# Placing the values of a second attention: by token and 25 small DMAs, or by a block-diagonal copy, transposes and small copies

## What is computed

```python
x = x + tanh(g_xattn[0]) * L0_xattn(layernorm(x), ctx, ctx, mask)     # 16 heads of 64
x = x + tanh(g_ffn[0])   * L0_ffn(layernorm(x))                       # 3 cycles of a coupling net
x = x + tanh(g_xattn[1]) * L1_xattn(ctx, layernorm(x), mask)          # 16 heads of 16
x = x + tanh(g_ffn[1])   * L1_ffn(layernorm(x))                       # shared expert + top 2 of 8 experts

def L1_xattn(src, tgt, attention_mask, Wq, Wk, Wv, Wo):
    q = heads(tgt @ Wq.T); k = heads(src @ Wk.T); v = heads(src @ Wv.T)
    scores = where(attention_mask, q @ k.T / sqrt(16), -inf)
    return merge(softmax(scores) @ v) @ Wo.T
```

## Time and profile before

| | us |
|---|---|
| median of 3 runs | 793.06 (792.92 to 800.51) |
| the profiled execution | 793.08, of which the span of its instructions is 791.3 |
| busy in the span: PE | 750.0 |
| PEld | 507.1 |
| DVE | 413.3 |
| ACT | 253.2 |
| POOL | 120.4 |

### The profile page before, as it was taken

The page is one execution under the profiler, slowest core; times in us unless marked ns, Lnnn a source line. Parts: engine busy times, 40 slices in busy tenths (PEclk is TensorE's granted clock), DMA queues, the critical chain, the costliest instruction groups (busy, mean ns, idle before and its releaser), DMA issues. The chain is left out here.

```text
span 791.3 us, 11353 instructions
## 1 busy us (share of the span) xinstructions
PE 750.0 (95%) x3378; PEld 507.1 (64%) x3379; DVE 413.3 (52%) x987; ACT 253.2 (32%) x542; POOL 120.4 (15%) x129
## 2 busy tenths in 40 slices
PE   7989999999899998799999999999999999999992
PEld 6856677667654444578888856556566566566661
DVE  5868766677723667976766635122333333333340
ACT  1532222222344444456566522111112122121220
POOL 4100000000000000000000103660132232322322
PEclk9999999999999999999999999999999999999996
DMA  9444000000032000047000201222223223232221
GB/s 304 132 135 136 0 0 1 0 0 0 1 119 94 0 1 0 1 167 260 0 0 1 81 1 69 101 100 74 42 40 48 46 43 50 40 47 47 41 39 20
DMA packets 38720, 45.09 MB, mean 57 GB/s; under 512 B 4212, under 2 KB 32454, under 8 KB 38692
## 3 DMA queue, kind: packets, MB, share of 16 engines
q1 hardware_dynamic: 31348, 34.99, 14.0%
q0 software_dynamic: 7344, 9.75, 7.5%
HBM read 27.91 MB, written 16.79 MB: 56 GB/s over the span
## 5 line engine op out<-in xcount | busy, mean ns | idle before, releaser
L399 PE MATMUL ps<-middle,work 128*128 128x256 f32 (+3 forms) x824 | 217.7, 410 | 2.2 <-ACT work L956 1.5
L956 ACT ACTIVATE work<-ps 128x256 f32<-128x256 f32 (+5 forms) x276 | 99.1, 412 | 364.9 <-PE ps L402 344.6
L399 PEld LDWEIGHTS ps<-middle,work 128*128 128x128 f32 x824 | 152.1, 190 | 42.5 <-issue 23.6
L399 PE MATMUL ps<-early,work 128*128 x312 | 141.1, 595 | 0.8 <-ACT work L956 0.8
L402 PEld LDWEIGHTS ps<-consts_sb,work 128*128 128x128 f32 (+1 forms) x672 | 76.7, 140 | 47.8 <-issue 26.4
L399 PE MATMUL ps<-late,work 128*128 128x34 f32 (+5 forms) x576 | 102.8, 331 | 3.6 <-ACT work L956 3.6
L402 PE MATMUL ps<-consts_sb,work 128*128 128x128 f32 (+1 forms) x672 | 93.8, 276 | 11.9 <-ACT work L956 4.7
L399 PEld LDWEIGHTS ps<-early,work 128*128 128x128 f32 x312 | 57.8, 190 | 61.7 <-issue 60.5
L399 PEld LDWEIGHTS ps<-late,work 128*128 128x128 f32 x576 | 81.2, 191 | 18.0 <-issue 8.9
L363 POOL TENSOR_TENSOR rstd<-var_eps,minus_half 128x8 f32<-128x8 f32 (+2 forms) x8 | 13.4, 1671 | 433.0 <-DVE var_eps L1266 433.0
L399 PE MATMUL ps<-early,late 128*128 128x512 f32 (+2 forms) x192 | 78.9, 615 | 0.0
(11 more groups left out here) (158 smaller groups left out, 607.1 us busy)
## 6 DMA issues: line engine op xcount, KB each, us to landing
early<-in_w SPq DMA_DIRECT2D x16, 512.0 KB, 10.1
expert_rows<-work SPq DMA_DIRECT2D x39, 130.0 KB, 2.7
work<-expert_rows SPq DMA_DIRECT2D x39, 130.0 KB, 2.1
middle<-in_w SPq DMA_DIRECT2D x8, 512.0 KB, 8.3
x_rows<-in_x SPq DMA_DIRECT2D x4, 512.0 KB, 9.6
out_rows<-x_rows SPq DMA_DIRECT2D x4, 512.0 KB, 3.4
late<-in_ws SPq DMA_DIRECT2D x3, 512.0 KB, 4.5
early<-in_wv SPq DMA_DIRECT2D x1, 1024.0 KB, 9.1
```

The lines of the kernel that those rows point to most:

```text
L399: return nc.tensor.matmul(o, l, r, start=start, stop=stop, **kw)
L956: return nc.scalar.activation(o, i, ACT.Copy)
```

## The change

The value projection is computed with tokens on the partitions (77 rows, 2 x 256 columns, bank 7), DVE copies it in one instruction to `vtok` (region `work`, 77 rows), and SP moves the rows of each head to their place in `va` by 25 DMAs (one for each head, and one more wherever a head crosses a chunk's end), both batches in one. POOL zeroes `va` in setup, and DVE waits for that before it writes the ones. PE's wait on `su1_t` becomes waits on `ones_done` and on all 25 DMAs. The block-diagonal copy, its memsets, the transposes and ACT's copies are gone. The 25 DMAs stand on SP behind the loads of `w2s` and ahead of those of `w13`.

```diff
@@ block.sync, after the loads of w2s
+            sp.wait_ge(q["su1_dve"], 2)
+            for h in range(H):
+                for c in range(NK * h // P, (NK * h + NK - 1) // P + 1):
+                    a, z = max(NK * h, P * c), min(NK * h + NK, P * c + P)
+                    sp.dma_start(va[a - P * c:z - P * c, :, c, h - heads_of(c)[0], 0:HD],
+                                 vtok[a - NK * h:z - NK * h, :, HD * h:HD * h + HD]).then_inc(q["ld_va"], 16)
@@ block.gpsimd, after the memset of mlhs
+            nc.gpsimd.memset(va.rearrange("p b c h e -> p (b c h e)"), 0.0).then_inc(q["va_fill"], 1)
@@ block.tensor, su1(w)
-                for m in range(2):
-                    for k in range(KD):
-                        last = mm(ps[:, 7, PW * m:PW * m + PW], (wk1s, wv1s)[w][:, k, P * m:P * m + P], ctx[:, k, :],
-                                  k == 0, k == KD - 1)
+                if w == 0:
...
+                else:
+                    for b in range(B):
+                        for k in range(KD):
+                            last = mm(ps[0:NK, 7, D * b:D * b + D], ctx[:, k, NK * b:NK * b + NK], wv1s[:, k, :],
+                                      k == 0, k == KD - 1)
@@ block.tensor, behind the net
             net3(5)
-            pe.wait_ge(q["su1_dve"], 2)
-            su1_turn(0)
             to_rows(1, 0, 4)
             to_rows(1, 1, 5)
             net4(5)
-            su1_turn(1)
...
-            pe.wait_ge(q["su1_t"], B * KC)
+            pe.wait_ge(q["ones_done"], B)
+            pe.wait_ge(q["ld_va"], 16 * (H + KC - 1))
@@ block.scalar
             act3(5)
-            act.wait_ge(q["ones_done"], B)
-            su1_turned(0)
             act4(10)
-            su1_turned(1)
             act4(11)
@@ block.vector
+            dve.wait_ge(q["va_fill"], 1)
             for b in range(B):
                 v.tensor_copy(va[:, b, :, :, HD], ...
@@ block.vector, su1_build(w)
+                else:
+                    last = v.tensor_copy(vtok.rearrange("p b d -> p (b d)"), ps[0:NK, 7, :])
@@ block.vector, in the loop of updates
                 if n == 3:
                     su1_build(0)
-                    for a, z in ((0, ZL), (ZL + HALF, Z1)):
-                        seq.mark(v.memset(z1[:, :, :, a:z], 0.0))
                 if n == 5:
-                    seq.sync()
                     su1_build(1)
```

More of the change, by code:

```diff
@@ L25 @@
 ZN = PAIRS * ZS + P
-ZL = 104
-Z1 = ZL + HALF + 48
 G4 = 512
@@ L105, in after @@
         eng.wait_ge(sem, value)
-def halves_of(c):
-    h0, n = heads_of(c)
-    return sorted({h0 // 8, (h0 + n - 1) // 8})
 def quarters(ap):
@@ L172, in build @@
         zv = cut(early, 8192 + B * PAIRS * PW, [B, ZN])
-        z1 = cut(work, 1536, [B, 2, Z1])
+        vtok = cut(work, 1536, [B, D])[0:NK]
         w13 = cut(early, 0, [NE, 2, KD, F])
@@ L248, in build @@
         dve_seq act_seq pool_seq var_done rstd_done memset_done gate_done
-        su_mm su_kv su_crow su_crow_bf su_g_mm su_g su_v_mm su_v bo_done ones_done su1_mm su1_dve su1_tm su1_t mask_done mrow_done
+        su_mm su_kv su_crow su_crow_bf su_g_mm su_g su_v_mm su_v bo_done ones_done su1_mm su1_dve va_fill ld_va mask_done mrow_done
         seed_mm seed_row n_xn n_tx n_xt n_sc n_sub n_exp n_p n_tp n_pt n_pv n_res
@@ L460, in su1 @@
                 pe.wait_ge(q["f_a4"], 2 * w + 3)
-                for m in range(2):
-                    for k in range(KD):
-                        last = mm(ps[:, 7, PW * m:PW * m + PW], (wk1s, wv1s)[w][:, k, P * m:P * m + P], ctx[:, k, :],
-                                  k == 0, k == KD - 1)
-                last.then_inc(q["su1_mm"], 1)
[L467 to L475, removed]
+                if w == 0:
+                    for m in range(2):
+                        for k in range(KD):
+                            last = mm(ps[:, 7, PW * m:PW * m + PW], wk1s[:, k, P * m:P * m + P], ctx[:, k, :],
+                                      k == 0, k == KD - 1)
+                else:
+                    for b in range(B):
+                        for k in range(KD):
+                            last = mm(ps[0:NK, 7, D * b:D * b + D], ctx[:, k, NK * b:NK * b + NK], wv1s[:, k, :],
+                                      k == 0, k == KD - 1)
+                last.then_inc(q["su1_mm"], 1)
             def xt(i, k, pre):
@@ L980, in _ @@
                                      ACT.Copy, scale=gate[:, 0:1]).then_inc(q["su_v"], 1)
[L982 to L992, removed]
             def ev_xt(i, k, pre, used):
@@ L1336, in su1_build @@
                 dve.wait_ge(q["su1_mm"], w + 1)
[L1337 to L1342, removed]
+                if w == 0:
+                    src = ps[:, 7, 0:2 * PW].rearrange("p (m b t) -> p m b t", m=2, b=B)
+                    for b in range(B):
+                        for m in range(2):
+                            last = v.tensor_tensor(kb1[:, b, m, :].rearrange("p (h t) -> p h t", h=8),
+                                                   spread(src[:, m, b, :], 1, [P, 8, NK]),
+                                                   spread(con[:, C_BD:C_BD + 8], 2, [P, 8, NK]), ALU.mult)
+                else:
+                    last = v.tensor_copy(vtok.rearrange("p b d -> p (b d)"), ps[0:NK, 7, :])
                 last.then_inc(q["su1_dve"], 1)
```

## The result

| | before | after |
|---|---|---|
| median, us | 793.08 (790.77 to 801.01, 20 runs) | 800.9 (795.04 to 805.34, 20 runs) |
| profiled execution, us (span) | 793.08 (791.3) | 801.58 (799.6) |
| granted TensorE clock over the span, its share of full speed | 0.990 | 0.973 |

The ratio is 1.0063, 95% interval 1.0039 to 1.0088: slower, by less than 1%. The medians differ by 7.8 us and the means by 5.6, since each kernel's runs fall into groups with different clocks. The forecast was 791.15 in a range of 788.5 to 794.2.

A forecast was written before the change was run, and what follows sets the result against it. PE was taken as the bound, busy 95% of the span, but in the seam PE's late `to_rows(1, 0)`, then DVE. Terms -2.23 - 0.40 + 0.70 = -1.93 took 793.08 to 791.15 us, range 788.5 to 794.2.

The forecast's parts named there:

- DVE's gap, -2.23: Seam, 304 to 317: DVE's idle time before `ffn_out(1, 0)` goes, since PE does `to_rows(1, 0)` earlier; -2.23 us.
- The second gap, -0.40: Before 323.74: DVE's idle time waiting for `to_rows(2, 0)` on PE closes; -0.40 us.
- `su1(1)`, +0.70: Value projection in the net: eight records of 256 instead of 154 columns, where PE has no slack; +0.70 us.
- DVE's copy at 0.75 us: Net: DVE's one 77x512 copy takes 0.75 us, all covered by PE, so it costs 0.
- The memset at 0.9 us: Setup: POOL zeroes `va` in 0.9 us, ending at 10.4; DVE comes at 19.57, so it costs 0.
- The 25 DMAs: On idle SP: 0.49 us per issue, last down at 295.5, PE needs them at 314.0; cost 0.
- The rival of late rows: Seam: uneven spread over engines makes PE wait for the DMAs at 314.0; decides from 64 ns per packet; chance 0.06.
- the cover of 1.6 us: Seam: PE's first scores are ready 1.6 us before DVE's softmax asks; without it the gain shrinks one for one.
- the price taken: DMAs landing late in the seam at 93 ns per packet, half way between 57 and 129: 14.2 us late, 803.8 us.
- The whole passage: Rival, seam: both turns leave PE, 3.16 us each, and all of it is gained: 787.5 us; chance 0.07.
- the swallowed gain: Rival, first tiles: PE's waits for ACT grow by what is gained, leaving 793.8 us; sign: longer waits; chance 0.13.
- The forecast's own range: Range of the main forecast, 789.8 to 793.0, said to come from the value projection's bounds and 1.6 us cover; chance 0.74.

The follow-up runs named there:

- e2_fill_two: Changed kernel plus 22 useless TensorE transposes behind `net4(5)` and 14 more behind `to_rows(2, 1)`, in the next hole: 797.8 us, ratio to before 1.0036.
- e1_fill: Changed kernel plus 22 useless TensorE transposes of the identity matrix behind `net4(5)`, in the 3.32 us hole: 795.4 us, ratio to before 1.0005.
- e6: Kernel before plus two useless matmuls of 208 columns (0.7 us) behind `su1(1)`, nothing else changed: 801.9 us, ratio to before 1.0085.
- e15: Kernel before plus twelve useless matmuls of 256 columns (5.1 us) behind `su1(1)`: 805.7 us, ratio to before 1.0152.
- e4: Kernel before plus four useless matmuls of 256 columns (1.7 us) behind `su1(1)`: 807.1 us, ratio to before 1.0154.
- e6_shift07: Full name of e6: kernel before plus two useless matmuls of 208 columns (0.7 us) behind `su1(1)`: 801.9 us.
- e10_fill29: Changed kernel plus 29 useless TensorE transposes behind `net4(5)`, filling the hole nearly whole: 796.1 us, ratio to before 0.9996.

## Why the prediction was wrong

**The step that failed** is one that the sum never made: its durations came from one execution with PEclk 1.00 in the seam and behind it (up to 486, in the windows above), and every later stage was taken over at that clock. No term and no rival had the granted clock. The range of before's own three runs, 792.92 to 800.51, stood in the table and was not asked about; before's 108 later runs, whose clocks are known, show the very same effect (790.5 at 0.992, 801.5 at 0.978). Since the median clock went from 0.990 to 0.973, the missing term is 17 x 0.69 = 11.7 us; with the 790.0 at equal clock that makes 801.7, and 800.9 was measured. (The 790.0 was itself obtained with this slope, so the agreement is a sum and no second proof; the 3.5 us between the two kernels at clocks from 0.977 to 0.982 is independent of it.) That the change stays within 1% had a chance of 0.94 and came true by luck: the gain was there, and the clock took more than it gave.

**DVE's gap, -2.23: right.** It is gone, and `ffn_out(1, 0)` follows the statistics. From the last row of `update(9)` (305.82; 305.67 before) to the softmax it is 12.06 us in place of 13.92: 1.86 gained, with a wait of 0.51 us for scores that the halved clock made late. At the full clock, in e2_fill_two, it is 2.32.

**The second gap, -0.40: right at the full clock.** It is 0.83 us in the execution after, with PE at half clock shortly before. In e1_fill (321.60) and e2_fill_two (321.94) it is closed, and the latter has `ffn_out(2, 0)` 2.80 us earlier, where 2.63 was forecast.

**`su1(1)`, +0.70: right**, 0.68 by the timeline. That it would cost only itself was wrong, as e6 shows.

**DVE's copy at 0.75 us: 0.69. The memset at 0.9 us, ending at 10.4: right, and DVE didn't wait.**

```profile
9.51 0.97 POOL L358 MEMSET late<- 128x1020 f32 x1
```

**The 25 DMAs: hidden, as forecast, but mis-sized.** One issue took 0.84 us (21.11 / 25) and not 0.49, so the last was issued at 301.04 and not by 293. The rival of late rows fell: the queue's view of the stretch 279 to 306 has

```profile
q1 hardware_dynamic: 2666, 0.16, 6.4%
```

which is 0.064 x 16 x 27 / 2666 = 10.4 ns for a packet, far under the 64 ns from which it would have decided. (Its price at 129 ns, 822 us, leaves out the cover of 1.6 us that the price taken has; with it the sum is 821.2.) The uneven spread by the Trainium skill, "DMA: Bandwidth & Descriptors", section "Why a DMA increments its semaphore by 16 and not by 1", would make 484 x 10.4 ns = 5.0 us on the busiest engine, an estimate by that page; no run shows the spread.

**The sum, -1.93.** Three readings: at 0.990 the change is worth 790.0 - 793.0 = -3.0 us, carried outside its runs; at clocks from 0.977 to 0.982 it is -3.5, from runs alone; e1_fill says -2.2 at 0.990, with the same gain and 2.6 us of filler in the hole. By the rows of e2_fill_two it is -2.80 + 0.68 = -2.1. So the mechanism of the gain held, and its size is right to about 1 us. The whole passage (787.5) and the swallowed gain (793.8) are not borne out: the former has PE and not DVE as the bound of the seam, the latter would leave nothing at equal clock, and in e2_fill_two the scores of 326.36 and 335.22 keep the gain. The sign that was named for the swallowed gain, longer waits of PE, was ill chosen: PE's wait is 3.29 us in e1_fill although the scores behind it come 2.32 us earlier, because PE is there earlier still. The forecast's own range, 789.8 to 793.0, doesn't follow from the bounds of `su1(1)`, which give 790.4 to 792.2, and the rest isn't derived.

**What stays open.** Why a given arrangement is favoured. Hole and shift each go with a lower clock and don't add up, and e15 took 4.8 us less than if e4's loss had come back in full. The place of a stage isn't fixed by the code alone either: in the 16 profiled executions PE reaches `su1(1)` between 275.72 us (e6_shift07) and 278.24 us (e10_fill29), over PE work that none of the edits touches, and with PEclk between 0.97 and 1.00 from 219 to 275. That spread is larger than the shift of 0.7 us, so one execution can't tell where a shift puts the seam. Shown is that the loss is the clock's, that it needs no hole, and that it isn't the DMAs.

## What to carry to other kernels

Where TensorE is busy 95% of the span, add a term for the granted clock to every sum: list all runs with their clock, fit time against clock, and compare kernels at equal clock before explaining a difference. A gain of 2 us in one seam is smaller than what most small moves did here: three of four mere shifts of the kernel before made it slower by 0.9 to 1.5%, the smallest by 0.7 us of harmless work. Compare with the kernel before in the same batch, and don't read one profiled execution as the typical one. When a critical wait is removed, look also at what the other engine does with its new idle time: PE's hole of 3.32 us behind the seam was the gain's other side.

## What was not expected of the hardware

- A busy TensorE stage runs at the lower clock in one execution and not in another of the same kernel: before's 108 runs spread over 11 us, 790.5 at a granted clock of 0.992 to 801.5 at 0.978.
- 0.7 us of added work cost 8.4 us against the pooled median of before, 1.7 us cost 13.6, and 3.4 us cost 3.4. The Trainium skill, "TensorE: Matmul & The Clock Gate", section "What's actually happening", says that the clock gate looks at the activity on a beat that runs on by itself and isn't reset by a kernel's start. The runs are in keeping with it, in that the time goes up and down again with the shift; none shows the beat.
- Adding 22 useless transposes made the changed kernel 5.5 us faster in the median, and brought no gain in a variant of it.
- The clock fell behind a wait of PE of 2.28 us in e6_shift07 and didn't behind the same wait in the kernel before.
